# Quantised feed-forward with a third product buffer, LayerNorm numbers computed a stage early, gate weights quantised in stage 1, one copy of the routed stage moved

## The reference

```python
x = x + _L0_xattn_ref(_layernorm(x), ctx, ctx, ...)    # 1 autocorrelation
x = x + _L0_ffn_ref(_layernorm(x), w_gate, w_up, w_down)  # 2 quantised FFN
x = x + _L1_xattn_ref(...)                             # 3 windowed attention
x = x + _L1_ffn_ref(...)                               # 4 soft slots, 8 experts
x = x + _L2_xattn_ref(...)                             # 5 full attention
x = x + _L2_ffn_ref(...)                               # 6 receptance FFN
x = x + _L3_xattn_ref(...)                             # 7 rotary attention
x = x + _L3_ffn_ref(...)                               # 8 routed FFN, top 2 of 8
```

```python
x = act_qdq(x)                                  # 16 bits, one scale for the tensor
up = act_qdq(x @ lpbq_dequant(w_up).T)          # weights: 4 bits, a scale per 32
gate = act_qdq(x @ lpbq_dequant(w_gate).T)
sig = fixed_qdq_u16(jax.nn.sigmoid(gate))
gate = act_qdq(gate * sig)
o = act_qdq(gate * up)
return o @ lpbq_dequant(w_down).T
```

## Time and profile before

| | us |
|---|---|
| median of 3 runs | 2160.91 |
| lowest, highest | 2156.86, 2163.7 |
| the profiled execution's own time | 2156.95 |
| its span in the trace | 2154.8 |
| stage 2 in the trace | about 122 to 326 |

### The profile page before, as it was taken

One profiled execution on the slowest core, in us unless ns is written; L12 is line 12 of the kernel. 1 busy time (PEld: TensorE's weight loads), 2 busy tenths in 40 slices (PEclk: granted clock), 3 DMA queues, 4 the chain that ended last, 5 costly groups with the idle time before them and its releaser, 6 DMA issues. The chain is left out here.

```text
span 2154.8 us, 40850 instructions
## 1 busy us (share of the span) xinstructions
PE 1865.7 (87%) x16258; PEld 1345.9 (62%) x16258; DVE 1478.9 (69%) x3056; ACT 1116.7 (52%) x1888; POOL 157.5 (7%) x122
## 2 busy tenths in 40 slices
PE   7949269894799999999999999889787797499995
PEld 7924145673377666677777666556564476398884
DVE  6677874556777777777777776836556565688886
ACT  3425753445356566665666565344441454367772
POOL 0001300001000000000000000000000000135441
PEclk9969689996999999999999999999988898599998
DMA  4010001002100000000000000000001000477775
GB/s 143 1 50 1 0 1 50 2 2 90 40 21 21 21 27 34 21 21 21 21 20 21 2 1 1 22 29 2 22 0 53 1 2 26 152 238 251 248 249 184
DMA packets 79451, 113.68 MB, mean 53 GB/s; under 512 B 9696, under 2 KB 62624, under 8 KB 79136
## 3 DMA queue, kind: packets, MB, share of 16 engines
q1 hardware_dynamic: 74848, 99.01, 14.1%
q0 software_dynamic: 4416, 12.06, 1.5%
HBM read 100.83 MB, written 10.22 MB: 52 GB/s over the span
## 5 line engine op out<-in xcount | busy, mean ns | idle before, releaser
L2344 PE MATMUL sl_ps_eo<-sl_w,sl_hT 128*128 128x256 f16 x3072 | 353.2, 273 | 0.8 <-DVE sl_hT L2582 0.7
L2321 PE MATMUL sl_ps_h<-sl_slot_inT,sl_w 128*128 128x512 f16 x1536 | 338.7, 380 | 0.5 <-ACT sl_h L2458 0.5
L2344 PEld LDWEIGHTS sl_ps_eo<-sl_w,sl_hT 128*128 128x128 f16 x3072 | 298.4, 98 | 35.9 <-DVE sl_hT L2582 1.3
L2458 ACT ACTIVATE sl_h<-sl_ps_h,sl_b1T 128x512 f32<-128x512 f32 x256 | 175.7, 687 | 170.0 <-PE sl_ps_h L2321 162.9
L2321 PEld LDWEIGHTS sl_ps_h<-sl_slot_inT,sl_w 128*128 128x128 f16 x1536 | 150.4, 98 | 176.3 <-issue 1.4
L2582 DVE TENSOR_TENSOR sl_hT<-sl_h,sl_hT 128x512 f16<-128x512 f32 x256 | 177.0, 692 | 102.1 <-ACT sl_hT L2461 97.8
L950 DVE TENSOR_REDUCE at_neg_max<-at_ps 128x8 bf16<-128x1024 f32 x96 | 117.0, 1221 | 144.2 <-PE at_ps L687 144.2
L1889 PE MATMUL mo_ps_h<-mo_xgT,mo_w 128*128 128x256 f16 x1104 | 128.0, 277 | 5.4 <-issue 4.2
L1900 PE MATMUL mo_ps_eo<-mo_w,mo_hT 128*128 128x256 f16 x1104 | 124.1, 273 | 0.0
L1889 PEld LDWEIGHTS mo_ps_h<-mo_xgT,mo_w 128*128 128x128 f16 x1104 | 109.5, 100 | 20.9 <-issue 6.6
L2593 DVE SCALAR_TENSOR_TENSOR sl_result<-sl_ps_eo,sl_b 128x256 f32<-128x256 f32 x128 | 54.3, 424 | 97.6 <-PE sl_ps_eo L2344 93.3
(11 more groups left out here) (385 smaller groups left out, 3631.1 us busy)
## 6 DMA issues: line engine op xcount, KB each, us to landing
mo_w_raw<-in_L_ffn_W SPq DMA_DIRECT2D x46, 1024.0 KB, 7.4
sl_w_in<-in_L_ffn_w SPq DMA_DIRECT2D x16, 1024.0 KB, 5.3
at_ctxT<-ctxT SPq DMA_DIRECT2D x9, 512.0 KB, 6.9
mo_w_raw<-pair_rows SPq DMA_DIRECT2D x4, 1024.0 KB, 9.0
mo_b<-in_L_ffn_b SPq DMA_DIRECT2D x23, 128.0 KB
at_wT<-L_attention_w SPq DMA_DIRECT2D x9, 256.0 KB, 7.0
ac_ctx_all<-in_ctx SPq DMA_DIRECT2D x4, 512.0 KB, 7.3
x_rows<-mo_xrow SPq DMA_DIRECT2D x4, 512.0 KB, 2.9
```

The lines of the kernel that those rows point to most:

```text
L2321: last = pe.matmul(ps_h[:, j % 2], w1[:, e % 2, w, k, j * P:(j + 1) * P], slot_inT[:, q % 2, x, k].rearrange("p b s -> p (b s)"), start=(k ...
L2344: last = pe.matmul(ps_eo[:, b % 2, 0:D], hT[:, hp, j, b * P:(b + 1) * P], w2[:, e % 2, w, j], start=(j, a) == (0, 0), stop=(j, a) == (HJ - ...
L2458: act.activation(h[:, j % 2], ps_h[:, j % 2], ACT.Gelu, bias=b1T[:, q // G4, j:j + 1], scale=1.0 / W_SCALE).then_inc(h_ready, 1)
```

## The change

It has seven parts.

1. LayerNorm numbers ahead. `Ahead` holds mean and 1/sqrt outside the stages. At the end of stages 1, 3, 5 and 7 DVE computes those of tiles 0 to 11 (`normal_ahead`: 12 `bn_aggr` and the links), ahead of `add_pair(7)` in stage 1 and in iteration n = 15 of the attention loop, ahead of `restate(12)`. The next stage begins with normalising, and `normal_rest` (4 `bn_aggr` and the links) stands further on: in stage 2 after tile 11, in stage 4 ahead of row 12 of x, in stage 6 after `mix(1)`, in stage 8 ahead of tile 12. Stages 3, 5 and 7 begin as before.
2. Gate weights. Their load stands in stage 1 behind `wo` and ahead of the later context loads, and their six quantising instructions in iterations 2 to 5 of its loop (`GateWeights`); stage 2 has neither.
3. `weights_low` of the gate weights' third tile stands behind `normal_rest`; the memsets stand behind the first `normal_x`.
4. `round_x` and `low_x` go by halves of the tokens: 2 and 2, then 2 and 2.
5. A one-column sigmoid stands after the last gate eviction on ACT, and up product 0 is evicted after `sigmoid(0)`, no longer ahead of it.
6. Five `round_up`, no longer four, stand ahead of the first `round_silu`; `prodT` and `prod_r` are three deep (the third in spare parts of `xqT`).
7. In stage 8 `tokens_out(1)` stands ahead of the last `w2_out` of tile 0; other tiles keep their order.

```diff
+AHEAD = 12
+def normal_ahead(dve, t, env, nth, stats_known, value, rows_only=False):
+    env.ahead.rows_only = rows_only
+    dve.wait_ge(stats_known, value)
+    layernorm_part(dve, t, env.ahead, nth, 0, AHEAD)
+def normal_rest(dve, t, env):
+    layernorm_part(dve, t, env.ahead, 0, AHEAD, B)
...
+class GateWeights:
...
+    def quantise(self, dve, piece):
...
+        if piece == 0:
+            dve.wait_ge(self.loaded, 16)
+            link(dve.tensor_reduce(self.maxima[:], w, AX.X, ALU.max, apply_absolute_value=True))
+            link(dve.tensor_scalar(self.scale[:], self.maxima[:], 1.0 / WQMAX, 1e-12, ALU.mult, ALU.max))
+            link(dve.reciprocal(self.inv[:], self.scale[:]))
+        elif piece == 1:
+            link(dve.tensor_tensor(w, w, self.inv[:].unsqueeze(2).to_broadcast(wide), ALU.mult))
...
@@ autocorrelation
             load_weight(wo, "wo", wo_in)
+            env.gate_weights.load(sp)
             for g in range(1, G4):
...
                 if j + 3 < NPAIRS:
                     normal_pair(j + 3)
+                if 2 <= j < 6:
+                    env.gate_weights.quantise(dve, j - 2)
+            normal_ahead(dve, t, env, 2, restated, AHEAD)
             add_pair(NPAIRS - 1)
@@ attention
                 if n + 1 < B:
                     maxima(n + 1, 1)
+                if n == AHEAD + 3:
+                    normal_ahead(dve, t, env, 1, restated, AHEAD, rows_only=windowed)
                 if n >= 3:
                     restate(n - 3)
@@ receptance_ffn
+            normal_group(0)
             dve.memset(xT[:, :, :, :, 0:1], 0.0).then_inc(zeroed, 1)
-            layernorm_begin(dve, t)
-            normal_group(0)
...
             mix(1)
+            normal_rest(dve, t, env)
             key(0)
@@ quantised_ffn
-UP_OUT = (((0,), (1,)), ((2,), (3,)), ((4, 5), ()), ((6, 7), ()), ((8, 9), ()), ((10, 11), ()))
+UP_OUT = (((), (0, 1)), ((2,), (3,)), ((4, 5), ()), ((6, 7), ()), ((8, 9), ()), ((10, 11), ()))
+RINGS = 3
+UP_FIRST = 5
...
             def product_parts(n):
-                enough(act, prodT_ready, n - 1)
+                enough(act, prodT_ready, n + 1 - RINGS)
...
-                enough(act, out_made, n - 1)
-                act.activation(prodT[:, n % 2, 0], low_half(prod_r[:, n % 2]), ACT.Copy).then_inc(prod_high, 1)
+                enough(act, out_made, n + 1 - RINGS)
+                act.activation(prodT(n)[:, 0], low_half(prod_r[:, n % RINGS]), ACT.Copy).then_inc(prod_high, 1)
...
+            act.activation(spare_sig[:], constant[:, 1:2], ACT.Sigmoid).then_inc(table_loaded, 1)
             act.wait_ge(x_ready, G4)
...
-                if n == 7:
-                    for piece in range(4):
-                        quantise_weights(0, piece)
-                if n == 11:
-                    weights_low(0)
+                if n == AHEAD - 1:
+                    weights_low_tile(0)
+                    weights_low_tile(1)
+                    normal_rest(dve, t, env)
+                    weights_low_tile(2)
...
-            for g in range(G4):
-                round_x(g)
-            for g in range(G4):
-                low_x(g)
+            for half in range(2):
+                for g in (2 * half, 2 * half + 1):
+                    round_x(g)
+                for g in (2 * half, 2 * half + 1):
+                    low_x(g)
...
-            product_low(0)
-            product_low(1)
+            for n in range(RINGS):
+                product_low(n)
             for n in range(B):
                 add_output(n)
-                if n + 2 < B:
-                    product_low(n + 2)
+                if n + RINGS < B:
+                    product_low(n + RINGS)
                 restate(n)
@@ routed_ffn
+                    if m == 0 and j == HJ - 1:
+                        tokens_out(1)
                     if j in (5, 7):
                         w2_out(m, (j - 5) // 2)
-                if m + 1 < NTILES:
+                if 1 <= m < NTILES - 1:
                     tokens_out(m + 1)
@@ slot_ffn
+                if m == FIRST_SLOT + E + AHEAD - B // 2 - 2:
+                    normal_rest(dve, t, env)
```

More of the change, by code:

```diff
@@ L98, in layernorm_begin @@
 def layernorm_begin(dve, t):
[L100 to L112 removed]
+    layernorm_part(dve, t, t, 0, 0, B)
 def layernorm_tiles(t, env):
@@ L1494, in _ @@
                     weights_high_tile((6, 8)[c])
-            for c in range(4):
+            for c in range(UP_FIRST):
                 round_up(c)
@@ L2762, in build_program @@
         env.early = Early(nc, ctx, env)
-        for phase in PHASES:
+        env.ahead = Ahead(nc, ctx)
+        with ExitStack() as first:
+            env.gate_weights = GateWeights(nc, first, env)
+            for phase in PHASES[:2]:
+                phase(nc, env)
+        for phase in PHASES[2:]:
             phase(nc, env)
```

160 lines of the change are left out of this document (89 added, 71 removed).

## The result

| | before | changed |
|---|---|---|
| median, us | 2160.16 (4 runs) | 2145.32 (4 runs) |
| lowest to highest | 2156.86 to 2163.70 | 2143.47 to 2145.54 |
| ratio, with its 95% interval | | 0.9929 (0.9912 to 0.9946) |
| span of the profiled execution | 2154.8 | 2141.6 |

The forecast was 2145.0, within 2137 to 2152. The medians differ by 14.8 us and the profiled spans by 13.2; the sum had 15.9.

What follows compares the result with a forecast made beforehand. The kernel was taken as serial at stage borders, bounded by whichever engine ends a phase last, in stage 2 DVE or ACT. Terms summed to -15.9 us, taking the median from 2160.91 to 2145.0; 2137 to 2152 held 8 in 10.

Steps and rivals of the forecast that it cites:

- Head of stage 2: From stage 2's barrier to the scale of x: LayerNorm numbers, gate quantising and idle go, `normal_rest` comes in; -9.1 us.
- Halves: `round_x` and `low_x` two and two in stage 2: PE's gate products start earlier, -0.9 us, ends 0 and -1.4.
- Sigmoid: Stage 2, gate rounding to first sigmoid: table load and eviction leave; DVE's chain up to 2.3 us earlier, taken as -1.9.
- Third buffer: Stage 2 output loop: addition, high half, low half, `restate`, next output still close a 4.5 us ring, 0; far end 3.7 us.
- Stage 1: Gate weights' six quantising instructions fit DVE's idle in four iterations: 0, with +3 us as the end.
- Stage 6: Head of stage 6: first normalising moves to the barrier, `normal_rest` falls into an idle of 3.48; -3.7 us.
- Stage 4: Head of stage 4: time gained only lengthens the wait for constants, `normal_rest` delays the next row; +0.6 us, ends 0 and +2.9.
- Stage 8: Head gives 0 behind a constant; PE's 3.11 us wait for the second routed tile falls by a w2 half, -1.1 us.
- Tails: `normal_ahead` at stage ends: hidden in stages 1 and 3, 0.1 us each in stages 5 and 7; +0.2.
- Covers partly lost: Rival: four pieces in stage 1 and tails of stages 3, 5, 7 each about 0.7 us late; 2150, chance 0.14.
- Slower: Rival: 20.6 us moved into stages 1, 3, 5, 7 isn't hidden, against 15.9 saved; +4.7 us, 2165.6, chance 0.03.
- The clock: Rival: three PE bursts (gate, output loop, stage 6) shift 2 us each; about 2141 or 2149, chance 0.10 on either side.

## Why the prediction was right, and where it wasn't

- **Head of stage 2**, -9.1: -9.25. `normal_rest` cost its 2.8 and the gate weights their 6.95 (7.1 when put back); the identity held nobody up. The sum had left out DVE's memsets, 0.33 us ahead of the LayerNorm numbers before, which the change also moved.
- **Halves**, -0.9: -0.78, and +0.77 when undone.
- **Sigmoid**, -1.9: this step failed, with -0.84 in the first trace and +0.9 in six others. I took DVE's chain to start as much earlier as ACT does, since DVE was waiting for POOL and POOL for ACT. That last link held before by chance: the sigmoid ended 7.0 us behind the scale, and the clamp, which is to be had 6.7 to 7.5 behind it, began at 7.07. In the first trace the stretch still lost 0.84, by a collision that fell well; in six of eight it is 0.9 longer than before. That the profiled execution had one of the two short ones is luck; which of the lengths the other runs of the changed kernel had isn't known. My row for this was the earlier trace rows, and I read a release from it without asking what POOL's own earliest start was.
- **Third buffer**, 0: the same turn of 4.54, and 0.04 us in the loop. The ring was as described, and opening its statistics link gave 3.2 us, near the 3.7 I had put as the far end.
- **Stage 1**, 0: the two traces differ by 1.8, but not by the change. With two product buffers and everything of the change in stage 1, it took 122.49. The difference is in the granted clock. The same eight matmuls near the start, in the changed kernel and in the one with two buffers:

```profile
14.77 3.62 PE L335 MATMUL ac_ps_q<-ac_wq,ac_specT 128*128 128x256 f32 x8 [1.21 <-ACT ac_specT L419]
```
```profile
14.36 1.97 PE L335 MATMUL ac_ps_q<-ac_wq,ac_specT 128*128 128x256 f32 x8 [1.21 <-ACT ac_specT L419]
```

  The trace's first record of the full clock begins at 18.13 us in the first and at 12.62 in the second, so the slow eight ran at the lower level and the fast eight at the full one. (A mean clock of this stretch shows 1.00 in both, since nothing is recorded ahead of that.) In all fourteen executions the eight took 1.96 or 1.97 us where that record begins by 14.4, and 3.52 to 3.75 where it begins behind 18.
- **Stage 6**, -3.7: -3.54 at the key, and -3.4 to -4.5 in the others that keep the part. **Stage 4**, +0.6: +0.55 at `inputs_rest`. The wait for constants took the whole head, as put.
- **Stage 8**, -1.1: -1.05 ahead of tile 1, and 1.4 to 2.2 at ACT's copy for tile 2 (77.42 and 77.50 without the part, 75.3 to 76.0 with it). The rest is the clock, which the term didn't have. Without the part the 48 matmuls of tile 1 took 7.07 us, and the granted clock was at its lower level for 3.4 us of them; behind the shorter wait they took 5.40 at the full level in nine of the twelve executions that have the part, and some 7.1 again in the other three, with the lower level once more. At the end of the stage the gain isn't to be seen: the stage took 341.78 and 347.44 us without the part, and with it 340.2 to 344.5, or 347.47 with the LayerNorm numbers at the heads. ACT's waits in the changed kernel's routed loop (us in total, times, longest):

```profile
ACT mo_w L2001 <- DMA mo_w_raw<-in_L_ffn_W: 17.9, 15, 2.7
```

  Weights that land late pace the loop in places, and by other amounts in each execution: the same total is 9.0 to 20.7 us over the fourteen. Whether the 2 us survive them on the mean stays open.
- **Tails**, +0.2: too small for the traces, in which stages 5 and 7 vary by 1.6 and 3.8 us.
- **Covers partly lost**: the gate weights cost as much in stage 2 as they take, and stage 1 without them took 124.08 us, beside 124.20 to 124.54 in the seven kernels with them whose first matmuls were slow as well. Next to nothing of them was paid there.
- **Slower**, the rival with 20.6 us of moved work: none of that work showed. With the LayerNorm numbers back at the heads, stages 3, 5 and 7 took 170.55, 160.24 and 192.00 us, no less than with them.
- **The clock** was the rival nearest to what happened: stages 1, 6 and 7 differ by 1.5 to 3.8 us between executions of kernels that are alike there. Stage 7 had 22 to 26 us at the lower level in four of the five executions of it below 190 us, and 29 to 33 in the seven of 192.0 or more.

## What to carry to other kernels

A wait in a trace names what ended last, not what would have ended next: before an instruction is counted as earlier, ask for the own earliest start of each engine in its chain. A further buffer pays only if the ring it lengthens is the one that closes; look which release PE really waits for, and whether it needs the whole of it. Work moved ahead of a barrier is free if its cover is measured in that iteration, and useless if the next stage's head waits for a load.
